# One GNN kernel: the banks of two products, the place of an accumulation in TensorE's step, and the semaphore that frees a gather slot

## The reference, cut to what matters

```
xn = layernorm(x)                                   # 6250 nodes, 256 channels
x  = x + gnn(xn) + mix(xn)                          # mix: linear attention and a feed-forward
x  = x + moe(layernorm(x))                          # 8 experts, top 1

def gnn(x):                                         # 200,000 edges, sorted by dst, 8 heads of 32
    h     = x @ W.T
    enc   = relu(edge_attr @ edge_W.T + edge_b)     # per edge, 256 values
    alpha = (h[src]*a_src).sum + (h[dst]*a_dst).sum + (enc*h[dst]).sum     # per head
    alpha = leaky_relu(alpha, 0.2)
    ex    = exp(alpha - segment_max(alpha, dst)[dst])
    out   = segment_sum(h[src]*ex, dst) / segment_sum(ex, dst) + bias
```

## Time and profile before

| | |
|---|---|
| Median of three runs | 4141.2 us (4132.48 to 4142.43) |
| Profiled execution | 4141.2 us, its span 4139.4 us |
| TensorE busy | 3496.6 us, 84% |
| VectorE busy | 2597.6 us, 63% |
| ScalarE busy | 2103.2 us, 51% |
| GpSimd busy | 2154.6 us, 52% |
| DMA packets | 449.27 MB, mean 109 GB/s |
| Mean granted TensorE clock | 0.942 of full |

### The profile page before, as it was taken

One profiled execution on the slowest core, in us unless ns is written; L12 is line 12 of the kernel. 1 busy time (PEld: TensorE's weight loads), 2 busy tenths in 40 slices (PEclk: granted clock), 3 DMA queues, 4 the chain that ended last, 5 costly groups with the idle time before them and its releaser, 6 DMA issues.

```text
span 4139.4 us, 88906 instructions
## 1 busy us (share of the span) xinstructions
PE 3496.6 (84%) x22054; PEld 2355.6 (57%) x22055; DVE 2597.6 (63%) x6056; ACT 2103.2 (51%) x5703; POOL 2154.6 (52%) x2172
## 2 busy tenths in 40 slices
PE   4788899959988888889888988889889859909999
PEld 2447788835555555555554555555555548708888
DVE  5757655547877777777777777777777744401121
ACT  2312233326666666666666666666666634413232
POOL 3302000046777777777777777777777701061111
PEclk8999999979999999999999999999999989959999
DMA  4631011135555555555555555555555530021110
GB/s 150 201 124 48 28 32 34 35 93 127 138 138 138 141 139 140 141 139 142 141 140 137 138 143 142 143 141 143 143 145 146 141 120 28 21 63 36 35 39 25
DMA packets 352302, 449.27 MB, mean 109 GB/s; under 512 B 170970, under 2 KB 275163, under 8 KB 350456
## 3 DMA queue, kind: packets, MB, share of 16 engines
q0 software_dynamic: 95568, 267.78, 26.1%
q10 hardware_dynamic: 108050, 122.83, 9.7%
q1 hardware_dynamic: 148231, 53.53, 5.4%
HBM read 389.57 MB, written 55.13 MB: 107 GB/s over the span
## 4 chain that ended last, share of the span: by engine, by line
PE 60%; SPq 11%; DMA 10%; issue 9%; DVE 4%; ACT 2%; ACTq 2%; POOL 2%; POOLq 0%; DVEq 0%
PE bank L1099 13%; PE bank L1040 10%; SPq L420 5%; PE bank L1185 5%; PE bank L1197 5%; PE bank L1145 4%; PE bank L1005 4%; PE bank L1061 4%; PE bank L1014 4%; SPq L423 3%; DMA link<-links 3%; DMA al<-h_tab,idx 2%; PE bank L1030 2%; SPq L412 2%; PE bank L918 1%
## 5 line engine op out<-in xcount | busy, mean ns | idle before, releaser
L514 POOL DMA_INDIRECT al<-h_tab,idx x976 | 1056.4, 1082 | 302.6 <-issue 296.3
L514 POOL DMA_INDIRECT gbuf<-h_tab,idx x784 | 854.4, 1090 | 405.5 <-issue 392.2
L1040 PE MATMUL bank<-oneh_t,hbt 125*128 125x512 bf16 x2640 | 670.7, 392 | 147.9 <-DVE prod L1462 144.6
L752 ACT ACTIVATE enc<-bank,eb 128x512 f32<-128x512 f32 x880 | 552.9, 680 | 260.0 <-issue 177.5
L1462 DVE SCALAR_TENSOR_TENSOR prod<-enc,adst,bank 128x512 f32<-128x512 f32 x880 | 629.5, 737 | 32.8 <-PE bank L1040 31.2
L1099 PE MATMUL bank<-msg,oneh 128*125 128x264 f32 x2352 | 610.4, 404 | 15.3 <-DVE r L1551 7.0
L770 ACT ACTIVATE dist<-iota_n,dtile 128x125 f32<-128x125 f32 x1760 | 551.1, 384 | 1.6
L1040 PEld LDWEIGHTS bank<-oneh_t,hbt 125*128 x2640 | 235.3, 99 | 468.1 <-issue 276.2
L1099 PEld LDWEIGHTS bank<-msg,oneh 128*125 128x125 f32 x2352 | 429.7, 193 | 112.1 <-issue 43.3
L1061 PE MATMUL bank<-prod,hsel 128*32 128x128 f32 x7040 | 293.9, 286 | 123.2 <-issue 122.9
L1061 PEld LDWEIGHTS bank<-prod,hsel 128*32 128x32 f32 x7040 | 173.9, 111 | 323.3 <-issue 322.6
(11 more groups left out here) (255 smaller groups left out, 5492.8 us busy)
## 6 DMA issues: line engine op xcount, KB each, us to landing
dstb<-dst ACTq DMA_DIRECT2D x440, 125.0 KB
al<-pen_d SPq DMA_DIRECT2D x1760, 4.0 KB
att<-attrx ACTq DMA_DIRECT2D x880, 24.0 KB
al<-h_tab,idx POOLq DMA_INDIRECT x976
link<-links SPq DMA_DIRECT2D x880, 0.2 KB
gbuf<-h_tab,idx POOLq DMA_INDIRECT x784
attrx<-al ACTq DMA_DIRECT2D x8, 1176.0 KB, 12.3
hsplit<-hb POOLq DMA_DIRECT2D x25, 375.0 KB, 5.9
```

The lines of the kernel that those rows point to most:

```text
L514: pool.indirect_dma_start(slot(n)[:, c, :], None, h_tab, bass.IndirectOffsetOnAxis(ap=idx[g % 2][:, k:k + 1], axis=0)).then_inc(gathered[n ...
L752: m = act.activation(enc[n % 2][:, k, :], bank[4 * (n % 2) + k][:, :], ACT.Relu, bias=eb[:, k:k + 1])
L1040: m = pe.matmul(bank[2 + k][:, :], hbt[:, ds(t & (HT - 1), 1), a, k * 128:(k + 1) * 128].rearrange("p t c -> p (t c)"), oneh_t[q][:, :], s ...
```

## The change

Four things change, all in the stage of the edges.

1. The encoding (`e_enc`, `e_relu`) uses banks 0 and 1 for every item, where it used 0, 1 and 4, 5 in turn. `e_enc(n)` accordingly waits for the relu of item `n-1`, not `n-2`.
2. The target rows (`e_dst`, `e_prod`) go to banks 2, 3 and 4, 5 in turn, where they went to 2 and 3. `e_dst(n)` waits for the product of item `n-2`, not `n-1`.
3. In TensorE's step, `e_enc` and `e_dst` come before `m_sum`, where they came behind it, and `e_enc` handles item `k` in step `k`, where it handled item `k+1`. The `e_enc(0)` ahead of the loop goes.
4. A gather slot is free once the message product of its former item is made (`msg_ready`), where it was free once TensorE had summed that message (`m_used`).

```diff
-                wait(pool, m_used, n - RING + 1)
+                wait(pool, msg_ready, n - RING + 1)
...
-                    m = act.activation(enc[n % 2][:, k, :], bank[4 * (n % 2) + k][:, :], ACT.Relu, bias=eb[:, k:k + 1])
+                    m = act.activation(enc[n % 2][:, k, :], bank[k][:, :], ACT.Relu, bias=eb[:, k:k + 1])
...
             def e_enc(n):
-                wait(pe, enc_ready, n - 1)
+                wait(pe, enc_ready, n)
...
             def e_dst(n, t):
-                wait(pe, prod_ready, n)
+                wait(pe, prod_ready, n - 1)
...
-            e_enc(0)
             for k in range(ITEMS + LM + 2):
...
+                if k < ITEMS:
+                    e_enc(k)
+                    e_dst(k, t[k % EB])
                 if 0 <= k - LM - 1 < ITEMS:
                     m_sum(k - LM - 1)
-                if k + 1 < ITEMS:
-                    e_enc(k + 1)
-                if k < ITEMS:
-                    e_dst(k, t[k % EB])
...
-                m = v.scalar_tensor_tensor(prod[q][:, k, :], enc[q][:, k, :], adst[:, k:k + 1], bank[2 + k][:, :], ALU.add, ALU.mult)
+                m = v.scalar_tensor_tensor(prod[q][:, k, :], enc[q][:, k, :], adst[:, k:k + 1], bank[2 + 2 * q + k][:, :], ALU.add, ALU.mult)
```

More of the change, by code:

```diff
@@ L1027, in e_enc @@
                 pe.wait_ge(item_in[b // 2], 96 * (n // EB) + 96)
-                wait(pe, enc_ready, n - 1)
+                wait(pe, enc_ready, n)
                 for k in range(KC):
-                    m = pe.matmul(bank[4 * (n % 2) + k][:, :], ew_bf[32 * k:32 * k + 24, k * 128:(k + 1) * 128], att[b][32 * k:32 * k + 24, :], start=True, stop=True)
+                    m = pe.matmul(bank[k][:, :], ew_bf[32 * k:32 * k + 24, k * 128:(k + 1) * 128], att[b][32 * k:32 * k + 24, :], start=True, stop=True)
                 m.then_inc(enc_mm, 1)
@@ L1036, in e_dst @@
                 pe.wait_ge(node_in, t * 16 + 16)
-                wait(pe, prod_ready, n)
+                wait(pe, prod_ready, n - 1)
                 for k in range(KC):
                     for a in range(3):
-                        m = pe.matmul(bank[2 + k][:, :], hbt[:, ds(t & (HT - 1), 1), a, k * 128:(k + 1) * 128].rearrange("p t c -> p (t c)"), oneh_t[q][:, :], start=(a == 0), stop=(a == 2))
+                        m = pe.matmul(bank[2 + 2 * q + k][:, :], hbt[:, ds(t & (HT - 1), 1), a, k * 128:(k + 1) * 128].rearrange("p t c -> p (t c)"), oneh_t[q][:, :], start=(a == 0), stop=(a == 2))
                 m.then_inc(d_ready, 1)
```

## The result

The changed kernel took 4192.7 us (median of four runs, 4185.5 to 4199.8), the kernel before 4139.4 us (4132.5 to 4142.4). The ratio is 1.0146, with a 95% interval of 1.0125 to 1.0168: **slower by 53 us**. In a second comparison it took 4205.0 against 4134.0 us, a ratio of 1.0172 (1.0150 to 1.0193). The direction was forecast; the time of 4305 us was not. The number is close to that of rival 1 (4198 us), but by luck: the experiments show that its reason is wrong too.

A forecast was written before the change was run, and what follows sets the result against it. Gathers bind at 22.17 us a group; the chain, 20.75 plus 0.2 (target tiles), 1.75 (relu wait) and 1.0 (clock), reaches 23.7. Over 107 groups that adds 164 to 4141.2 us: 4305 us, range 4170 to 4363.

The forecast's parts named there:

- rival 1: Edge stage: the engines' chain grows but TensorE's clock holds; +57 us, 4198 us; chance 0.25.
- What bounds the kernel before: Edge stage: GpSimd's back-to-back gathers bind at 22.17 us a group; the engines' chain, led by ScalarE, needs 20.75.
- The slot's semaphore: GpSimd's wait for gather slots: earlier release saves nothing in the steady stretch; price 0, bounds 0 and -5 us.
- the two sets of banks: Target rows: `e_dst` no longer waits for the previous item's product; absorbs single late tables, mean pace unchanged, price 0.
- +1.75 us in every group: ScalarE's first-step relu waits for TensorE's encoding, itself behind fac; added in full to the chain, bounds 1.2 to 2.0 us.
- So at full clock only the first step waits: ScalarE's relus in later steps find their encodings ready; no added wait there.
- The margins of 0.5 and 0.3 us: Time by which the encodings of the second and third steps were expected ready before ScalarE needs them.
- The clock: TensorE's pause before each first step grows to about 3 us, dropping its clock: 1.0 us a group, ends 0 and 1.55.
- What falls later eats the margins of 0.5 and 0.3: Low-clock slowdown falling after the piece ScalarE waits for uses up the later steps' spare time of 0.5 and 0.3 us.
- The sum: Edge stage: 23.7 us a group against 22.17, over 107 groups +164 us, giving 4305 us.
- Rival 3: Gathers speed up through a new rhythm of VectorE's message products; 131 us less, 4010 us; chance 0.08.
- What the profile was to show: Edge stage: fac to fac near 23.7 us, one relu wait a group, clock about 0.93, slot waits, hardly any `link` waits.

The follow-up runs named there:

- the late encoding alone: Kernel before, with only the first steps' encodings issued late, behind the wait for fac and the head sum: 4135.0 us, ratio 0.9998 to the kernel before.
- the filled pause: Changed kernel plus nine extra 128x128 products in TensorE's pause ahead of each first step: 4103.4 us, ratio 0.9915 to the kernel before.
- the encoding at the head: Changed kernel with item k's encoding at the very head of step k, ahead of the wait for fac: 4087.9 us, ratio 0.9892 to the kernel before.

## Why the prediction was right or wrong

**What bounds the kernel before: right, as far as tested.** The gathers' arithmetic holds in four kernels on the first kind of chip, all with GpSimd back to back. Sixteen times (mean gather in the stage + 0.30) gives 22.2, 22.2, 21.9 and 21.7 us for the kernel before, the late encoding alone, the filled pause and the encoding at the head; fac to fac was 22.17, 22.18, 21.89 and 21.63. The direct test, fewer gathers, has no run there.

**The slot's semaphore, the two sets of banks: priced at 0.** Not tested apart, but 0 was wrong for the order as a whole: with the encoding at the head its chain is 0.8 to 1.4 us a group faster at full clock. With the clock held or the encoding moved, the changed order is 32 to 46 us faster than the kernel before, and that comes from shorter gathers; why they are shorter is not shown.

**"The relu starts at about 1.8 instead of 0.06: +1.75 us in every group. ScalarE has no pause to swallow it." This is the step that failed.** The first half is right: 1.68 us after fac. The second is wrong. In the group shown, fac to the second relu went from 5.33 us to 6.19 (2007.70 to 2013.89), +0.86; the second step took 4.64 instead of 4.55, with the third relu's new wait of 0.74 in it; the rest was 0.15 shorter. At full clock this group takes 21.61 us against 20.82, and by the table above the full-clock groups grew by 0.2 to 0.6 us: **+0.8 us at most instead of +1.75**. ScalarE's steps held waits for TensorE already, for line 1064 in the first and, by the same sign, for line 1092 in the second (`dstb`'s load begins 1.05 us after the relu in the kernel before, 0.28 in the changed one). The profile lists no idle time for them, since the relu's end hid all but a few hundredths, and the long gap ahead of line 759 is put down to "issue". I took a row without idle time for a row that waits for nobody.

The size of what was swallowed depends on what it is measured against. On the kernel before, the late encoding costs the chain some 0.1 us. On the new order it costs 1.2 (medians, 20.2 to 21.4) to 1.6 (first groups, 19.68 to 21.32); there it is late in every step and not only in the first. The prediction added +1.75 and 0 to the old chain as if neither changed the other; for both together the runs have the 0.2 to 0.6.

"So at full clock only the first step waits" failed with it. The margins of 0.5 and 0.3 us were counted from an old first step of 5.27 us behind the relu. That step is now 4.51 us, since its old wait is gone, and so ScalarE comes earlier to the next encodings: in the group shown the second relu starts 0.04 us after its encoding is written (2013.46 + 0.39 to 2013.89), and the third waits 0.74. TensorE works through without a pause from the head sum to the last `m_sum`, 18.4 us (2007.96 to 2024.42 + 1.95) and not 19.2, and in the first three steps ScalarE follows it.

**The clock: right in kind, sized at 1.0.** It costs the chain 1.3 to 1.4 us a group and the kernel at least 0.9. The prediction took 1.0 of 1.55 us, since some groups would escape. Some did, 32%, but the other 68% lost 1.9 us each in their first step, more than the 1.55 read from the earlier trace rows for a shorter piece of work. "What falls later eats the margins of 0.5 and 0.3" is not what happened: behind the second relu nothing more was lost.

**The sum.** Forecast: 20.95 + 1.75 + 1.0 = 23.7. Measured: 21.35 + 1.43 = 22.78. (The second line is the mean of the full-clock groups plus what the others add to it, so it comes out by its making; the part that is measured another way is the clock's, at least 0.9 by the filled pause.) What made the change three times too large, +164 us against +53, is the chain at full clock: the full-clock groups, tile loads included, stand at 21.35, where 22.7 was forecast. That is the +1.75 of the hand-over and the 0 of the other parts together, 1.35 us too much. 1.35 x 107 is 144 us, and the forecast missed by 112; the clock term was 0.4 x 107 = 46 us short the other way, and the rest is the earlier first fac and the difference between the trace and the median.

**Rival 1** gave 4198 us for a chain of 22.7 at full clock. The time is near by luck, and both of its halves are wrong: the clock does not hold, and where it is made to hold the kernel takes 4103. **Rival 3**, the gathers' rhythm, is real, at 0.3 to 0.5 us a group; in the changed kernel it lay hidden under the clock's cost.

**What the profile was to show.** Right: the relu waits (though in all four steps: 97 in first steps, 81, 58 and 50 in the others), the pause of about 3 us, the clock of 0.93, the waits for slots, the end of the waits for `link`. Wrong: 23.7 us fac to fac with little spread (22.78, and two kinds of groups 2 us apart), and one relu wait a group (2.8).

## What to carry to other kernels

Before a new wait is added to an engine's chain in full, look for the waits for the same engine that already stand a few instructions behind it: they show as no idle time when another instruction's tail covers them, and the new wait may take their place: here 1.5 us of it cost the old chain some 0.1. When a change gathers TensorE's idle time into one longer pause, price the lower clock behind it as a term of its own, and test it by filling the pause; here nine useless products were worth more than the change had cost. That is a test and not yet a remedy: on the other kind of chip they won nothing, and one execution of that kernel took 5372.6 us; whether the added products had a part in it is not known. And move an instruction that others wait for ahead of its own engine's waits, not just earlier in the step: the encoding before `bank7_read` and not behind the head sum made 117 us of difference on the first kind of chip, and none on the other.

## What the runs showed of the hardware

- A gather that begins inside VectorE's product of two operands in SBUF ends 0.82 to 0.91 us after it, as the earlier trace rows showed for one: 415 of 1695 gathers of the kernel before do, and take 1.48 us in the mean, the others 0.96. With the encoding at the head it is 425 of 1691 and 1.38 us, so they begin later inside the product. That moves the mean gather by 0.03 us, which is 0.5 us a group where gathers bind.
- GpSimd's gather starts 0.78 us after the end of the VectorE instruction whose semaphore it most likely waits for (33 places), of which 0.30 us stand ahead of every gather; TensorE starts 0.10 us after fac.
- Chips differ: on some, what waits for TensorE in the same program starts later, a waiting relu of the changed kernel 2.8 us after its encoding in the median and up to 10, and a change that costs 1.5% on one kind costs 7% on the other. A comparison across the kinds would have been worthless; each ratio here is to the kernel before on the same chip.
